# A decoder block on one core: in the first stage x1 is normalised on ACT with a bias from DVE, logits are copied later, and two loops are written out

## The reference

```python
x1 = layernorm(x + attn(x))            # v = x Wv^T; v * rotor; cumulative sum over t; turned back; times Wo^T
x2 = layernorm(x1 + xattn(x1, ctx))    # scores times a decay matrix, each row of ctx divided by max(|row sum|, 1)
out = layernorm(x2 + moe(x2))          # 8 experts, the top 2 of each token by softmax of the router's logits
# layernorm(x) = (x - mean(x)) / sqrt(var(x) + 1e-5) over the last axis
```

## Time and profile before

| | |
|---|---|
| time, median of 3 runs | 296.65 us (294.85 to 298.92) |
| span of the profiled execution, first to last instruction | 269.3 us |
| median less that span (start and end outside the trace) | 27.35 us |
| first stage in the trace | about 0 to 110 us |
| experts in the trace | about 125 to 236 us |
| last stage in the trace | about 236 to 269 us |

### The profile page before, as it was taken

The page is one execution under the profiler, slowest core; times in us unless marked ns, Lnnn a source line. Parts: engine busy times, 40 slices in busy tenths (PEclk is TensorE's granted clock), DMA queues, the critical chain, the costliest instruction groups (busy, mean ns, idle before and its releaser), DMA issues.

```text
span 269.3 us, 5242 instructions
## 1 busy us (share of the span) xinstructions
PE 208.4 (77%) x1393; PEld 184.8 (69%) x1394; DVE 169.8 (63%) x534; ACT 116.8 (43%) x286; POOL 153.1 (57%) x140
## 2 busy tenths in 40 slices
PE   8387698988989998857899999999999999400000
PEld 8387587977978888757688888888888888300000
DVE  5945988889889768595355455455554554207993
ACT  4352251433424420381345545454554554515665
POOL 1264857747756720085567777777777774515330
PEclk9889999999999999995999999999999999855555
DMA  7945456656543100550223223233332332079413
GB/s 222 392 163 179 136 194 223 168 176 198 205 164 119 39 22 21 189 166 2 88 79 104 86 94 99 86 97 100 97 96 87 97 95 78 12 213 318 171 78 156
DMA packets 20130, 35.75 MB, mean 133 GB/s; under 512 B 2861, under 2 KB 11312, under 8 KB 20112
## 3 DMA queue, kind: packets, MB, share of 16 engines
q1 hardware_dynamic: 16368, 26.21, 29.6%
q0 software_dynamic: 3744, 9.31, 11.3%
HBM read 27.12 MB, written 9.31 MB: 135 GB/s over the span
## 4 chain that ended last, share of the span: by engine, by line
PE 62%; DVE 17%; issue 9%; POOL 4%; DMA 4%; ACT 2%; DVEq 1%; SPq 0%; ACTq 0%; POOLq 0%
PE p_c L558 13%; PE p_v L558 7%; PE p_y L480 6%; PE p_y L584 4%; PE p_r L558 4%; PE p_a L558 4%; PE p_s L464 3%; PE p_s L558 3%; PE p_v L420 3%; PE p_t L597 3%; POOL space L1020 3%; DVE space L851 3%; PE p_r L508 2%; PE p_a L499 2%; PE p_t L446 2%
## 5 line engine op out<-in xcount | busy, mean ns | idle before, releaser
L558 PE MATMUL p_c<-w_hi,parts 128*128 x104 | 34.6, 414 | 0.0
L1044 POOL DMA_INDIRECT y_dram<-x1T,scatter_now x26 | 26.3, 1013 | 11.8 <-issue 5.3
L1024 POOL DMA_INDIRECT turns<-x_dram,gather_now x26 | 25.4, 979 | 12.6 <-issue 3.8
L823 DVE TENSOR_TENSOR parts<-p_y,parts 128x256 fp32r<-128x256 f32 x39 | 16.5, 424 | 17.6 <-ACT parts L934 17.6
L1011 POOL TENSOR_TENSOR w_lo<-keep,w_hi 128x1536 fp32r<-128x1536 f32 (+1 forms) x8 | 27.5, 3434 | 0.1
L833 DVE TENSOR_TENSOR cs<-p_c,cs 128x256 f32<-128x256 f32 x26 | 11.0, 425 | 22.6 <-ACT cs L941 22.6
L994 POOL TENSOR_TENSOR space<-back 128x512 f32<-128x512 f32 x8 | 10.2, 1271 | 18.9 <-DVE back L717 18.9
L941 ACT ACTIVATE cs<-p_c 128x256 f32<-128x256 f32 x26 | 10.1, 387 | 24.6 <-PE p_c L558 24.6
L437 PE MATMUL p_c<-const,space 128*128 128x128 f32 x128 | 17.3, 292 | 4.2 <-DVE space L671 4.2
L664 DVE TENSOR_SCALAR x<-r,mv,rs 128x256 f32<-128x256 f32 x32 | 20.2, 671 | 0.6
L1002 POOL TENSOR_TENSOR cs<-space,vinv 128x256 f32<-128x256 f32 x16 | 9.5, 612 | 18.5 <-DVE vinv L731 15.0
(11 more groups left out here) (161 smaller groups left out, 575.0 us busy)
## 6 DMA issues: line engine op xcount, KB each, us to landing
keep<-in_weights SPq DMA_DIRECT2D x8, 768.0 KB, 4.4
space<-y_dram SPq DMA_DIRECT2D x16, 256.0 KB, 4.2
space<-in_xT SPq DMA_DIRECT2D x8, 256.0 KB, 3.5
keep<-in_x SPq DMA_DIRECT2D x8, 256.0 KB, 3.5
space<-in_ctxT SPq DMA_DIRECT2D x8, 256.0 KB, 2.8
space<-in_ctxt SPq DMA_DIRECT2D x8, 256.0 KB, 3.1
x_dram<-x SPq DMA_DIRECT2D x8, 256.0 KB, 2.2
keep<-x_dram SPq DMA_DIRECT2D x1, 2048.0 KB, 8.4
```

The source lines that it names most:

```text
L558: last = nc.tensor.matmul(dst, lhs[:, k, :], w[:].rearrange("p e n -> p (e n)")[:, bass.ds(start + col + k * width, width)], start=(n == 0 ...
L823: nc.vector.tensor_tensor(xs_lo[s], p_xt, xs_hi[s].bitcast(F32), ALU.subtract).then_inc(xlo_ok, 1)
L1024: nc.gpsimd.indirect_dma_start(xs[s], None, x2_dram, bass.IndirectOffsetOnAxis(ap=gather_now[s][:], axis=0)).then_inc(xs_ok[s], 16)
L1044: nc.gpsimd.indirect_dma_start(y_dram, bass.IndirectOffsetOnAxis(ap=scatter_now[s][:], axis=0), ys[s], None, bounds_check=TOPK * N - 1, oo ...
```

## The change

- DVE no longer computes x1. Behind the reciprocal `rs1` it computes `shift1` = -mean * rs1 for both halves in one scalar_tensor_tensor of 128x2 elements.
- ACT computes x1 as Identity(r1 * rs1 + shift1), in two instructions of 128x256, behind the square root sd1, and gives `x1_ok`.
- ACT copies the logits of pair i-3 behind the square root of step i, where before it copied those of pair i-2 at the end of step i. The last pair's copy stands behind the pipeline.
- DVE waits for `x1_ok` before it writes the next r1, since ACT still reads the old one; ACT waits for `r2_ok` before it overwrites the x1 buffer.
- `pipeline` has no loop any more: all steps are written out, in the first and in the last stage.

```diff
+        shift1 = sb("x1_shift", [P, 2])
@@ pipeline
-            for i in range(first, 2):
-                fixed(i)
-            with engine.Fori(1, PAIRS // 2 - 1) as half:
-                step(2 * half, 0, lambda k: True)
-                step(2 * half + 1, 1, lambda k: True)
-            for i in range(PAIRS - 2, PAIRS + 2):
+            for i in range(first, PAIRS + 2):
                 fixed(i)
@@ DVE step
                 if has(-1):
-                    normalise(i - 1, r1, mv1, sd1, rs1, x1[1 - s], sd1_ok, rs1_ok, x1_ok)
+                    dve.wait_ge(sd1_ok, i)
+                    nc.vector.reciprocal(rs1[:], sd1[:]).then_inc(rs1_ok, 1)
+                    dve.wait_ge(rs1_ok, i)
+                    nc.vector.scalar_tensor_tensor(shift1[:], mv1[:, :, 0], -1.0, rs1[:], ALU.mult, ALU.mult).then_inc(
+                        shift1_ok, 1)
@@
                 if has(0):
                     dve.wait_ge(y_ok, i + 1)
                     dve.wait_ge(x_ok[s], 8 * (i - s) + 16)
+                    if has(-1):
+                        dve.wait_ge(x1_ok, i)
                     nc.vector.tensor_tensor(r1[:], p_y[:], x_in[s], ALU.add).then_inc(r1_ok, 1)
@@ ACT
+            def copy_logits(j):
+                act.wait_ge(lg_ok, j + 1)
+                nc.scalar.activation(logits[:, bass.ds(2 * j, 2), :], plog, ACT.Copy).then_inc(logits_ok, 1)
+
             def step(i, s, has):
                 if has(-1):
                     act.wait_ge(mv1_ok, 2 * i)
                     nc.scalar.activation(sd1[:], mv1[:, :, 1], ACT.Sqrt, bias=eps[:]).then_inc(sd1_ok, 1)
+                if has(-3):
+                    copy_logits(i - 3)
+                if has(-1):
+                    act.wait_ge(shift1_ok, i)
+                    if has(-3):
+                        act.wait_ge(r2_ok, i - 2)
+                    for q in range(2):
+                        last = nc.scalar.activation(x1[1 - s][:, q, :], r1[:, q, :], ACT.Identity,
+                                                    scale=rs1[:, q:q + 1], bias=shift1[:, q:q + 1])
+                    last.then_inc(x1_ok, 1)
                     act.wait_ge(t1_ok, i)
                     nc.scalar.activation(x1T[:], p_t[:], ACT.Copy).then_inc(x1T_ok, 1)
@@
                     nc.scalar.activation(x2T[:], p_t[:], ACT.Copy).then_inc(x2T_ok, 1)
-                    act.wait_ge(lg_ok, i - 1)
-                    nc.scalar.activation(logits[:, bass.ds(2 * (i - 2), 2), :], plog, ACT.Copy).then_inc(logits_ok, 1)
 
             pipeline(act, step)
+            copy_logits(PAIRS - 1)
```

More of the change, by code:

```diff
@@ L284, in decoder_block @@
             "v_ok", "turned_ok", "sums_ok", "back_ok", "got_ok", "y_ok"))
-        r1_ok, st1_ok, mv1_ok, sd1_ok, rs1_ok, x1_ok = (sem(n) for n in (
-            "r1_ok", "st1_ok", "mv1_ok", "sd1_ok", "rs1_ok", "x1_ok"))
+        r1_ok, st1_ok, mv1_ok, sd1_ok, rs1_ok, shift1_ok, x1_ok = (sem(n) for n in (
+            "r1_ok", "st1_ok", "mv1_ok", "sd1_ok", "rs1_ok", "shift1_ok", "x1_ok"))
         t1_ok, x1T_ok, sc_ok, att_ok, sum_ok, vabs_ok, vmax_ok, vinv_ok, cs_ok, av_ok = (sem(n) for n in (
```

## The result

The changed kernel takes 303.23 us (median of 4 runs, 302.0 to 303.94), the kernel before 297.78 us (294.85 to 299.26, 4 runs). The ratio is 1.02 with an interval of 1.013 to 1.027: about 2% slower, 5.5 us by the medians. Forecast were +4.1 us and 300.8 us, with a range of 296.5 to 304.5.

A forecast was written before the change was run, and what follows sets the result against it. The first stage was taken as bound by a cycle through POOL, where x1 stood behind `w_lo`. The terms +5.3 - 0.5 - 0.7 = +4.1 us gave 300.75 us, 1.4% slower, range 296.5 to 304.5.

The forecast's parts named there:

- The hold of the shift: First stage: `shift1` on DVE, issued inside POOL's `w_lo`, is held and ends 0.02 us behind `w_lo`'s end.
- the two-input rule: Skill's rule: a Vector instruction with two SBUF inputs contends with a GpSimd instruction reading SBUF; whichever starts second blocks.
- +0.67 us a step: First stage: PE's transposes start 1.20 us behind `w_lo` instead of 0.53, for each step going round by POOL.
- How many steps: First stage: all eight pairs pay, seven at 0.67 us and pair 6 at 0.62, summing to +5.3 us.
- The logits copy at nothing: First stage: moving ACT's logits copy behind the square root changes 0, since the end of `w_lo` comes later anyway.
- Writing out, -0.5 and -0.7: Steps without loops: first stage saves 2 x 0.26 = 0.5 us, last stage 0.36 twice, 0.7 us.
- the 27 us: Whole kernel: shown median taken as 27.35 us above the profiled span, added to the forecast span of 273.4.
- Rival A: First stage: shift not held by `w_lo`, PE the bound, steps about 9.6 us; -6.1 us, 290.5 us; chance 0.08.
- B: Last stage: rival that it loses its collisions when written out, -4.0 instead of -0.7; +0.8 us, 297.5 us; chance 0.12.
- C: Slower rival: 0.80 us a pair, nothing back from loops, one more collision; +7.5 us, 304.1 us; chance 0.10.

## Why the prediction was right

**The hold of the shift.** Right: 2.15 us, ending 0.02 to 0.03 behind `w_lo`; expected was 0.02. For pairs 6 and 7, whose shift is issued later in `w_lo`, it is 0.93. It was read from one instruction of the last stage. One reading beside it was wrong: x1 was not under the two-input rule that the prediction quotes, for it has one tensor input in SBUF, and yet it was held. The forecast did not need it, since it went by the row of the shift.

**+0.67 us a step.** Right: the gap from `w_lo` to PE is 1.20, as summed, and steps are 11.4 apart, as forecast. The seven steps behind the first transposes take 80.13 us against 73.17; without the low clock's 2.75 (below) this is +4.2, where the forecast had +4.1.

**How many steps.** All eight, as forecast, but the first in another way. Its shift was issued at 21.28 and took 0.16 us, because that `w_lo` ended at 21.40 and there was next to nothing left to wait for. PE still started 1.22 us behind `w_lo` instead of 0.54, since x1 itself takes 1.09 us on ACT after a shift of 0.16, where DVE needed 0.73 in all. When that shift falls deeper into `w_lo`, as with the logits copy in its old place (issued 21.45, `w_lo` to 22.44), it is held too, for 1.00 us. The changed kernel's first pair in the timeline of 16 to 24 us:

```profile
17.96 3.44 POOL L1026 TENSOR_TENSOR w_lo<-keep,w_hi 128x1536 fp32r<-128x1536 f32 x1
...
21.28 0.16 DVE L708 SCALAR_TENSOR_TENSOR x_shift<-mv,rs 128x2 f32<-128x2 f32 x1
...
21.47 1.09 ACT L906 ACTIVATE x<-r,x_shift,rs 128x256 f32<-128x256 f32 x2 [0.43 <-DVE x_shift L708]
...
22.62 0.66 PE L442 MATMUL p_t<-const,x 128*128 128x128 f32 x4 [2.02 <-ACT x L906]
```

**The logits copy at nothing.** Right for this change, and for the reason given: with the hold gone it costs 0.23 us a step.

**Writing out, -0.5 and -0.7.** The first stage's steps became equal, as forecast. The last stage is 1.5 us shorter in the two profiles compared, but 0.8 in the mean of all profiles with and without loops, close to the term. In the time neither is found by itself.

**What the sum left out: the clock.** Two stretches in the changed kernel's first stage ran at a low granted clock. They account for 2.75 us, by comparison with the one profile with filled waits. Neither profile of before has one in its steps, though PE waits there too, 2.2 us at the longest. With +6.97 for that part of the trace against +4.1, this is nearly the whole miss there: 4.1 + 2.75 = 6.9. The prediction gave PE's idle time no price beyond its own length. In these profiles it had one in some executions; how often it is paid in the timed runs is not shown.

**What was misread: the 27 us.** The prediction said that the median lies 27.35 us above the span for work outside the trace. Every later run shows 1.8 to 2.1. The other 25 us were inside, in the experts' stage: 136 us or more in every later profile, 111 in the first. It did no harm, since no term came from that stage, but the warning was there: a sum of spans that leaves a tenth of the time unexplained. The stage's changes by 2 to 5 us from profile to profile also make the difference between +4.1, +5.5 (medians) and +6.1 (spans) hard to divide further.

**Luck.** That the sum came within 1.4 us of the medians' difference (4.1 against 5.5) is in part luck. The terms for the hold were right, but the clock (+2.75) was left out, and in the trace the -1.3 us ahead of the first transposes, which the change did not earn, and the longer gain of the last stage went against it.

Rival A was the right picture of a kernel without the hold, and wrong of this one. B did not happen: the last stage gained 1.5 at most, not 4. C's price of 0.80 a step did not either.

## What to carry to other kernels

When work is moved off DVE to escape a POOL instruction, count the small instruction that stays behind to feed it: it waits for the same thing, and the engine that now does the work starts later than the old one did. For each DVE instruction near a long POOL operation, find a row of the same form beside a POOL instruction in the trace. Here a scalar_tensor_tensor with two tensor inputs in SBUF was held at 128x2 and at 128x256 (the second expert's addition), and so was a tensor_scalar of 128x256; the tiny one, rewritten as two tensor_scalar of 128x1 with a per-partition scalar, cost 0.2 us more and was never held. And check that the profiled span and the timed runs agree before adding to either.

## What the runs showed of the hardware

- A DVE scalar_tensor_tensor of 128x2 with two SBUF inputs, issued while `w_lo` ran on POOL, ended 0.02 to 0.03 us behind it, after up to 2.15 us. A tensor_scalar of 128x1 with a per-partition scalar took 0.165 us at the same place, a reciprocal of 128x2 0.15. The hold ended at a boundary between two POOL instructions issued back to back. The Trainium skill ("SBUF — State Buffer", section "Who interferes with whom") says of two-input instructions what the trace shows.
- A DVE tensor_scalar of 128x256 with one tensor input was held as well: 2.16 us for the pair of x1 inside `w_lo`, 0.74 with POOL idle.
- The granted clock fell below 1.00 behind PE waits of 1.8 to 2.9 us in some executions and not in others (the kernel with written-out steps fell to 0.57 at 34 to 38 us behind a wait of 2.2 us; before, with the same wait, stayed at 1.00). In the one profile with all these waits filled it stayed at 1.00 throughout the first stage's steps. What decides between the two is not settled.
- The experts' stage took 111 us in one execution and 136 to 141 us in eleven others. What held it in the eleven was not tried; the profile names the releaser of some waits there only as "remote".
